# A wait ahead of each scatter of message tiles in a two-layer graph kernel

## What is computed

```python
edge_index = jnp.stack([src, dst])
h = jnp.maximum(_layernorm(x, axis=-1), 0.0)
x = x + _L0_gnn_ref(h, edge_index, L0_gnn_W_l, L0_gnn_W_r, L0_gnn_b)   # mean of neighbours, linear, log_softmax
h = jnp.maximum(_layernorm(x, axis=-1), 0.0)
x = x + _L1_gnn_ref(h, edge_index, edge_attr_64, ...)

# _L1_gnn_ref
weight = jnp.maximum(edge_rbf @ W1 + b1, 0.0) @ W2 + b2     # one row of 128 for each edge
h = x @ Wl + bl
msg = h[dst] * weight
out = jax.ops.segment_sum(msg, src, num_segments=x.shape[0])
```

## Time and profile before

| | us |
|---|---|
| median of 3 executions | 4677.88 |
| lowest, highest of these | 4672.25, 4679.68 |
| the profiled execution, whole | 4644.02 |
| its span, first to last instruction | 4642.2 |

### The profile page before, as it was taken

The page is one execution under the profiler, slowest core; times in us unless marked ns, Lnnn a source line. Parts: engine busy times, 40 slices in busy tenths (PEclk is TensorE's granted clock), DMA queues, the critical chain, the costliest instruction groups (busy, mean ns, idle before and its releaser), DMA issues.

```text
span 4642.2 us, 96340 instructions
## 1 busy us (share of the span) xinstructions
PE 3605.8 (78%) x24907; PEld 2626.4 (57%) x24908; DVE 2637.6 (57%) x7188; ACT 1823.9 (39%) x3754; POOL 1740.7 (37%) x1753
## 2 busy tenths in 40 slices
PE   2999999989877777777677677777777677778887
PEld 1666666657554455445455455555555445457776
DVE  7888888876444444444444444444444444457776
ACT  4666666643222222222222222222222222258887
POOL 2100000001255555555555555555555555520000
PEclk9999999995577777777777777777777777789999
DMA  3599600000023223332233333333332332258787
GB/s 90 183 318 316 212 5 6 6 1 10 23 78 76 77 76 76 78 76 77 76 76 77 76 77 76 77 77 75 78 76 77 77 76 76 76 150 223 224 225 211
DMA packets 572233, 468.65 MB, mean 101 GB/s; under 512 B 289293, under 2 KB 543334, under 8 KB 572181
## 3 DMA queue, kind: packets, MB, share of 16 engines
q1 hardware_dynamic: 515782, 348.95, 29.1%
q0 software_dynamic: 56400, 119.07, 7.5%
HBM read 235.79 MB, written 231.94 MB: 101 GB/s over the span
## 4 chain that ended last, share of the span: by engine, by line
PE 36%; another core or an unknown queue 27%; issue 18%; DVE 10%; ACT 5%; DVEq 2%; ACTq 1%; DMA 0%; POOL 0%; POOLq 0%; SPq 0%
PE PS L980 10%; PE PS L1092 5%; PE PS L1104 4%; PE PS L971 4%; DVE X L904 3%; PE PS L1081 3%; PE PS L1140 3%; DVE aux L659 2%; ACT big L1281 2%; PE PS L1073 1%; PE PS L1089 1%; ACT big L1269 1%; DVE H L893 1%; DVEq L899 1%
## 5 line engine op out<-in xcount | busy, mean ns | idle before, releaser
L492 POOL DMA_INDIRECT messages<-big,idxr x1664 | 1619.1, 973 | 1313.8 <-DVE big L865 811.4
L1104 PE MATMUL PS<-par,big 128*128 x4992 | 598.0, 268 | 753.1 <-ACT big L1281 706.7
L865 DVE TENSOR_TENSOR big<-PS,big 128x512 f32<-128x512 f32 x416 | 287.8, 692 | 1502.3 <-ACT big L1281 1142.5
L1104 PEld LDWEIGHTS PS<-par,big 128*128 128x128 bf16 x4992 | 479.6, 114 | 881.8 <-issue 805.4
L1281 ACT ACTIVATE big<-PS 128x512 f32<-128x512 f32 x416 | 248.4, 597 | 1325.3 <-remote 1121.3
L980 PE MATMUL PS<-par,aux 128*128 128x386 bf16 x3626 | 683.3, 327 | 0.0
L1092 PE MATMUL PS<-W2s,big 128*128 128x128 f32 x3328 | 678.1, 367 | 0.0
L1092 PEld LDWEIGHTS PS<-W2s,big 128*128 128x128 f32 x3328 | 576.6, 261 | 145.9 <-issue 145.9
L1202 ACT ACTIVATE aux<-PS 128x784 bf16<-128x784 f32 x592 | 479.7, 822 | 295.2 <-PE PS L971 288.2
L1269 ACT ACTIVATE big<-PS,b1c 128x512 f32<-128x512 f32 x416 | 284.4, 684 | 647.1 <-issue 424.5
L1140 PE MATMUL PS<-big,H 128*128 128x128 f32 x3456 | 444.0, 281 | 80.4 <-DVE H L893 64.1
(11 more groups left out here) (202 smaller groups left out, 3761.3 us busy)
## 6 DMA issues: line engine op xcount, KB each, us to landing
messages<-zeros SPq DMA_DIRECT2D x576, 193.5 KB
big<-messages SPq DMA_DIRECT2D x216, 516.0 KB, 3.7
aux<-slot_rows SPq DMA_DIRECT2D x416, 128.0 KB
big<-in_edge_attr_dram SPq DMA_DIRECT2D x1664, 32.0 KB
messages<-big,idxr POOLq DMA_INDIRECT x1664
X<-in_x_dram SPq DMA_DIRECT2D x6, 448.0 KB, 11.9
out_dram<-X SPq DMA_DIRECT2D x6, 448.0 KB
edge_places<-big SPq DMA_DIRECT2D x1, 2496.0 KB, 13.1
```

The lines of the kernel that those rows point to most:

```text
L492: pool.indirect_dma_start(strm_d, bass.IndirectOffsetOnAxis(ap=idxr[:, n % U, j:j + 1], axis=0), outr[:, n % U, j, :], None).then_inc(S_sc ...
L1104: last = nc.tensor.matmul(pHG[:, j * C:(j + 1) * C], oht[:, k % 2, j * P:(j + 1) * P], h1p[:, ds(at + a * C, C)], start=(a == 0), stop=(a ...
```

## The change

The semaphore of a scatter no longer belongs to its buffer but to its place `j` in the group. In the message stage POOL now waits ahead of each scatter, until the scatter with the same `j` of the group before has landed, and counts with one more register for each place. DVE's wait before it overwrites `idxr` is over all four semaphores, to the same landing as before (all scatters of the group four back and older).

```diff
-        S_sc = [sem(f"scattered_{k}") for k in range(U)]
+        S_sc = [sem(f"scattered_{j}") for j in range(J)]
...
+            landed_j = [pool.alloc_register(f"landed{j}") for j in range(J)]
...
                 for j in range(J):
+                    if not isinstance(g, int):
+                        pool.wait_ge(S_sc[j], landed_j[j])
+                        pool.reg_add(landed_j[j], landed_j[j], 16)
+                    else:
+                        wait(pool, S_sc[j], 16 * g)
                     pool.indirect_dma_start(strm_d, bass.IndirectOffsetOnAxis(ap=idxr[:, n % U, j:j + 1], axis=0),
-                                            outr[:, n % U, j, :], None).then_inc(S_sc[n % U], 16)
+                                            outr[:, n % U, j, :], None).then_inc(S_sc[j], 16)
...
+            for j in range(J):
+                pool.reg_mov(landed_j[j], 16 * U)
...
-                wait(dve, S_sc[k], (g - k) * 16)
+                for j in range(J):
+                    wait(dve, S_sc[j], 16 * (g - U + 1))
                 nc.vector.tensor_copy(idxr[:, k, :], place_f).then_inc(S["rank_chain"], 1)
```

## The result

The changed kernel takes 4689.89 us (median of 8 runs, 4687.93 to 4693.3), the kernel before 4678.56 us in the same comparison (8 runs, 4672.25 to 4680.43). The ratio is 1.0030, with a 95% interval of 1.0021 to 1.0038: slower by 11.3 us. The forecast was 4692.5 us, 14.6 us slower.

A forecast was written before the change was run, and what follows sets the result against it. Bound: the message stage's loop between engines, 13.72 us a pair of groups. One POOL register instruction, 0.07 us x 208 = 14.6 us, other terms nothing, on 4644.02 us plus 33.9 us gave 4692.5 us; range 4668 to 4712 us.

The forecast's parts named there:

- two irregular pairs: Message stage, about 3064 and 1440 us: first scatter's late start passed on nearly in full (14.47 us), delay inside burst not (13.78).
- The bound: Message stage: a 13.72 us loop per pair of groups through row copy, message product and POOL's first scatter; 208 periods, 2854 us.
- The wait does not block: POOL's scatters: the landing four places ahead, 5.1 us earlier, is met before it is asked, so nothing is held back.
- The instruction at the first scatter: POOL, behind the wait for messages: one register instruction on the loop, 0.07 us x 208 pairs = 14.6 us (6.7 to 25).
- DVE's waits cost nothing: DVE ahead of the write of idxr: three more semaphores, at most 0.2 us a group, covered by its pauses.
- What the profile would show: Changed profile: first scatter 0.86 us behind messages instead of 0.79, pair period 13.79 us, stage some 15 us longer.
- constant addition: Whole kernel: the median's 33.9 us over the profiled execution (4677.88 against 4644.02), taken as the same for the changed kernel.
- signs by which I would be wrong: Message stage: row copy's unnamed wait of 1064 us much changed, bursts breaking into fours, or POOL's waits naming a landing.
- Rival (a): PE's late signal not timed by POOL's burst, or instruction under 0.045 us: within 0.2%, 4678 to 4687 us; chance 0.35.
- Rival (b): Late signals go with POOL's bursts; if the pattern broke, 10.2 us a pair, 730 us less, 3950 us; chance 0.10.
- Rival (c): POOL's wait noticed late or queue not filled ahead: 0.49 us a first scatter, 102 us, 4780 us; chance 0.05.

The follow-up runs named there:

- dose_8b: Kernel before with eight more register instructions on POOL behind the wait for messages, no wait for a landing, on the slow chip: 1.0268, 125.7 us slower.
- dve_waits_b: Kernel before with three more waits on DVE ahead of the write of idxr, all met long ago, on the slow chip: 0.9994.
- half_scatters: Kernel before with two scatters a group instead of four, leaving out the messages of two tiles of four, on the slow chip: 3455.62 us, one execution.
- depth_2: Changed kernel with each scatter waiting for the landing of the scatter two ahead instead of four, on a quick chip: 1.2169 against the kernel before.
- dose_8: Kernel before with eight more register instructions on POOL behind the wait for messages, no wait for a landing, on a quick chip: 1.0002.
- pool_waits_only: Changed kernel with one DVE wait, for a landing one group later, in place of four; POOL's four waits kept; quick chip: 1.0056 against the kernel before.
- pool_waits_b: Second run of POOL's four waits with one DVE wait, for a landing one group later, in place of four; quick chip: 1.0050 against the kernel before.

## Why the prediction was right, and where it was not

The forecast of the time held, and the mechanism that it priced is the one that the runs show. One premise behind it fails on the rows of the kernel before. I wrote that a delay inside the burst is not passed on, from the pair about 1440 us, where the row copy came 11.47 us behind the first scatter in spite of the pause. The next first scatter, which I did not look at, does come late (timeline, POOL and DVE):

```profile
1454.78 0.96 POOL L492 DMA_INDIRECT messages<-big,idxr  x1 [2.88 <-DVE big L865]
...
1453.29 0.69 DVE L865 TENSOR_TENSOR big<-PS,big 128x512 f32<-128x512 f32 x1 [7.08 <-remote]
```

That is 1454.78 - 1440.27 = 14.51 us instead of 13.72, and 3.04 us behind its row copy. The pair of the earlier trace rows follows another of these pauses, and its first scatter is late for the same reason:

```profile
3052.76 0.97 POOL L492 DMA_INDIRECT messages<-big,idxr  x1 [3.81 <-DVE big L865]
3055.77 0.96 POOL L492 DMA_INDIRECT messages<-big,idxr  x1 [2.04 <-issue]
```

All 15 pairs with a pause behind the first scatter take 14.50 to 14.62 us, so half of a pause of 1.74 us is passed on, some 13 us in that profile. The two irregular pairs were one effect seen twice, and no evidence that the start of the burst alone sets the time.

- **The bound.** A loop over two groups, passed through by POOL's burst: shown. dose_8b delayed the first scatter by 0.61 us in the median, and the time grew by 0.60 us a pair. That the start of the burst sets the time, and not its end, is not shown; for the sum it makes no difference, since the added instruction moves both.
- **The wait does not block.** Right, by POOL's unchanged idle times. That only 2.2 us name a landing is weak evidence, with most records missing.
- **The instruction at the first scatter.** The term was 0.07 us a pair, 14.6 us. The first scatter starts 0.870 us behind the messages instead of 0.795, and one instruction costs 0.0755 us by dose_8b, 15.7 us in all. The whole change came to 11.3 and 10.7 us. The 15.7 us lie within both intervals (9.8 to 17.8 us and 7.5 to 15.9). The 4.6 us by which dve_waits_b lies below the kernel before would fill the gap (15.7 - 4.6 = 11.1), but that gain is not clear of noise and its waits are not those of the change. That POOL's waits alone make the loss on the slow chip is inferred from dose_8b, which has no landing in it, and dve_waits_b; it was not run as such.
- **DVE's waits cost nothing.** Right as far as the stand-ins tell, by 0.9994 on the slow chip.
- **What the profile would show.** Here a step failed: I wrote that the pair would take 13.79 us and the stage 15 us more. The changed profile has 14.0 and 43 us. The failed step is that I took the 34 us between the profiled execution of before and its median for a constant addition: that execution had short pairs, and the next one has not. The forecast of the time did not suffer, because the addition cancels in it: 4692.5 us is the median of before plus 14.6. Of the signs by which I would be wrong, two appeared: the row copy's wait for an unnamed releaser is 540 us and not 1064, and bursts break up now and then (of 207 steps from one burst's start to the next, 6 span one group and 5 span three). Both appear in dve_waits_b too (631 us, and 3 of 209 that span one), where POOL's program is that of before, so they were bad signs for the question. The third, a landing named as the releaser, came 5 times with 2.2 us.
- **Rival (a), no change:** both of its reasons fell with dose_8b, the price under 0.045 us and the signal timed by something else; the two measured losses are 0.30% and 0.25%. **Rival (b), faster:** the limit of four in flight did not change what is in flight, so it did not come to a test. half_scatters shows that its second half was sound: PE's late signals do go with POOL's scatters. What they are worth in the whole kernel is an estimate from the two kinds of chips: 4674 - 3918 = 756 us. **Rival (c):** not for this change; depth_2 shows its price where a wait does bind.
- **What I did not see at all:** that the bound I read from the trace is not there on every chip. On a quick chip the forecast's term is nothing (dose_8, 1.0002), and what then costs is a pause that is no longer covered (20 us by pool_waits_only and pool_waits_b), which stood in no case of mine.

## What to carry to other kernels

An instruction costs nothing or its whole time by where it stands: behind the wait that starts an engine's idle queue, one register instruction of 0.075 us was paid in full in each turn of the loop, and eight were paid eightfold; ahead of a full queue they are free. A wait for something that has nearly always happened already can still have two prices: its own time on an idle queue, and, as far as the untested reading of the pool_waits runs goes, the slots of the queue that it leaves empty, which then no longer cover a pause. Before a rule is drawn from two irregular pairs, follow each up to the start of the next pair, and count all pairs like it. Before a fraction of a per cent is explained from two single profiles, compare each profiled execution with its own median, and run the kernel before on more than one chip.

## What the runs showed of the hardware

- One kernel, two kinds of chips: 4673.62 and 4678.56 us against 3917.56, 3924.51 and 3917.58 us. On the slow kind PE's signals reach ACT some 5 us late once in two groups (1064 us of waits in all) and SP's four transfers take 6.24 us to issue in one group of two instead of 1.91. With half the scatters both get shorter (235 us, and 3.92 us at the longest), and neither appears on the quick chips. What it is in the chip, or whether it is the chip, the records do not tell.
- POOL makes a pause every 104 indirect transfers in the kernel before: a second scatter starts 3.01 us behind the first instead of 1.27, 15 times in 1664. dose_8b, with eight more register instructions a group, has it every 104 transfers too. With a full queue it is not visible.
- A scatter that waits for a landing starts 0.78 us behind the last of the 16 semaphore updates and 1.2 us behind the last packet, in the median (depth_2). A first scatter that waits for messages starts 0.79 us behind them, and one that follows in a queue needs 0.30 us of idle time.
- One register instruction with a wait that is already met, ahead of an idle queue of POOL, costs 0.0755 us (dose_8b: 125.7 us for 8 x 208).
